# Edge loop of a graph attention layer: the running sum as a plain addition, its source slot read from a table

## What is computed

```python
def gnn(x, src, dst, edge_attr):             # x: normalised
    q, k, v = (x @ W + b for each)           # [N, 8, 32]
    e = edge_attr @ We                       # [E, 8, 32]
    alpha = sum(q[dst] * (k[src] + e)) / sqrt(32)
    ea = exp(alpha - segment_max(alpha, dst)[dst])
    denom = segment_sum(ea, dst)
    msg = (v[src] + e) * (ea / denom[dst])
    return segment_sum(msg, dst) + x @ Ws + bs
x = x + gnn(layernorm(x))
x = x + moe_top2_of_8(layernorm(x))          # router, two experts per node, relu, 256 -> 512 -> 256
```

## Time and profile before

| | us |
|---|---|
| median of three runs | 2544.61 |
| the profiled execution's own time | 2543.3 |
| its span, first to last instruction | 2541.5 |
| PE busy | 2375.7 (93%) |
| DVE busy | 2029.1 (80%) |
| POOL busy | 1809.0 (71%) |
| ACT busy | 1573.9 (62%) |
| edge loop, first L1050 to last | 227.4 to 1927.0 |
| mean granted TensorE clock | 0.966 of full speed |

### The profile page before, as it was taken

The page is one execution under the profiler, slowest core; times in us unless marked ns, Lnnn a source line. Parts: engine busy times, 40 slices in busy tenths (PEclk is TensorE's granted clock), DMA queues, the critical chain, the costliest instruction groups (busy, mean ns, idle before and its releaser), DMA issues. The chain is left out here.

```text
span 2541.5 us, 61885 instructions
## 1 busy us (share of the span) xinstructions
PE 2375.7 (93%) x13314; PEld 1998.8 (79%) x13315; DVE 2029.1 (80%) x5248; ACT 1573.9 (62%) x4349; POOL 1809.0 (71%) x2136
## 2 busy tenths in 40 slices
PE   6998999999999999999999999999996658999998
PEld 3445888888888888888888888888884647999998
DVE  6865999999999999999999999999997873222222
ACT  1223677776777677777777777776775115666665
POOL 4213788888888888888888888888886204666666
PEclk9999999999999999999999999999998558999999
DMA  7326777777777777777778777777772672433443
GB/s 233 129 106 197 234 229 224 228 228 224 223 228 228 219 229 228 223 228 226 228 226 230 228 223 228 226 228 215 230 225 82 203 215 57 71 63 64 69 67 54
DMA packets 337727, 476.35 MB, mean 187 GB/s; under 512 B 61382, under 2 KB 268556, under 8 KB 337116
## 3 DMA queue, kind: packets, MB, share of 16 engines
q0 software_dynamic: 92576, 259.72, 38.4%
q1 hardware_dynamic: 238556, 213.23, 27.7%
q10 hardware_dynamic: 6288, 0.05, 0.1%
HBM read 425.40 MB, written 50.57 MB: 187 GB/s over the span
## 5 line engine op out<-in xcount | busy, mean ns | idle before, releaser
L809 POOL DMA_INDIRECT kv_ring<-vk_table,tab_c x880 | 860.0, 977 | 274.9 <-issue 176.5
L967 PE MATMUL ps_e<-we_sb,aT 128*128 128x256 f32 x3520 | 917.8, 384 | 23.8 <-DVE ve_ke L1055 19.9
L967 PEld LDWEIGHTS ps_e<-we_sb,aT 128*128 128x128 f32 x3520 | 602.0, 191 | 95.6 <-issue 46.3
L1050 DVE TENSOR_TENSOR ve_ke<-kv_ring,ps_e 128x512 f32<-128x512 f32 x880 | 599.7, 681 | 34.1 <-PE ps_e L971 22.7
L819 POOL TENSOR_TENSOR ve_ke<-ve_ke 128x256 f32<-128x256 f32 x880 | 551.2, 630 | 16.5 <-ACT factor L936 3.0
L1020 PE MATMUL ps_u<-ve_ke,sel 128*128 128x264 f32 x1760 | 545.3, 392 | 17.0 <-POOL ve_ke L819 6.1
L971 PE MATMUL ps_e<-q_slots,selT 128*128 x1760 | 517.5, 375 | 0.0
L896 ACT COPY aT<-ps_t 128x256 f32<-128x256 f32 x880 | 325.4, 370 | 294.6 <-PE ps_t L951 255.3
L1126 DVE SCALAR_TENSOR_TENSOR node_slots<-node_slots,same_tile,ps_u 128x264 f32 x880 | 422.6, 480 | 25.5 <-PE ps_u L1020 21.4
L971 PEld LDWEIGHTS ps_e<-q_slots,selT 128*128 128x128 f32 x1760 | 335.3, 191 | 45.1
L1038 DVE TENSOR_REDUCE alpha<-ve_ke 128x8 f32<-128x256 f32 x880 | 362.4, 412 | 1.9
(11 more groups left out here) (251 smaller groups left out, 2630.3 us busy)
## 6 DMA issues: line engine op xcount, KB each, us to landing
a_ring<-in_edge_attr SPq DMA_DIRECT2D x880, 128.0 KB
loc_c<-loc_table SPq DMA_DIRECT2D x220, 128.0 KB, 4.4
kv_ring<-vk_table,tab_c POOLq DMA_INDIRECT x880
vk_table<-kv_out SPq DMA_DIRECT2D x49, 256.0 KB, 2.0
skip_table<-skip_out SPq DMA_DIRECT2D x49, 128.0 KB, 1.7
skip<-skip_table SPq DMA_DIRECT2D x7, 896.0 KB, 9.3
xn_table<-node_slots SPq DMA_DIRECT2D x7, 896.0 KB, 5.1
w_sb<-in_L_ffn_W SPq DMA_DIRECT2D x2, 2048.0 KB, 10.3
```

The lines of the kernel that those rows point to most:

```text
L809: g.indirect_dma_start(out=kv_ring[:, i % N_KV, :], out_offset=None, in_=vk_table, in_offset=bass.IndirectOffsetOnAxis(ap=tab_c[:, c % N_T ...
L967: t.matmul(ps_e[i % 2][:, 0:D], aT[i % 2][:, k * P:(k + 1) * P], we_sb[:, k, :], start=(k == 0), stop=(k == KD - 1))
L1050: v.tensor_tensor(ve_ke[:, to:ke + 1:ke - to, 0:D], kv.rearrange("p (t d) -> p t d", t=2), e[:, None, :].to_broadcast([P, 2, D]), ALU.add) ...
```

## The change

The 0/1 factor goes out of the addition. A table made in the first stage gives for each item the pair (tile, source): source is the tile itself if the item before had the same tile, else NT + 2, a new slot behind the others whose 264 columns are zero. The table stands in two halves at partitions 64 and 96 of `item_rows`. The addition is a tensor_tensor of the source slot and `ps_u`. The registers are loaded for two items at once, four values, in `score` behind the key/value addition (L1050) of each item whose addition has an even index, that is at the odd items. In the drain, where there are no scores, the load stands ahead of the addition. Three small tables of the router stage and the output buffers `y` of the expert stage become parts of other buffers.

```diff
+        item_slots = [item_rows[64 + 32 * h:65 + 32 * h, :].rearrange("p (i k) -> p i k", k=2) for h in range(2)]
-        node_slots = sb("node_slots", [P, NT + 2, SLOT])
+        sums_flat = sb("node_slots", [P, (NT + 2) * SLOT + UW])
+        node_slots = sums_flat[:, 0:(NT + 2) * SLOT].rearrange("p (j w) -> p j w", w=SLOT)
...
+            from_rep = t_rep
...
                 g.memset(node_slots[:, 0, 0:UW], 0.0).then_inc(first_cleared, 1)
+                g.memset(sums_flat[:, (NT + 2) * SLOT:(NT + 2) * SLOT + UW], 0.0).then_inc(first_cleared, 1)
...
                 then(v.tensor_tensor(same_tile[:, 1:IT], node_tile_rep[:, 1:IT], node_tile_rep[:, 0:IT - 1], ALU.is_equal))
+                then(v.scalar_tensor_tensor(out=from_rep[:, :], in0=node_tile_rep[:, :], scalar=float(NT + 2), in1=same_tile[:, :],
+                                            op0=ALU.subtract, op1=ALU.mult))
+                for h in range(2):
+                    row, some = slice(64 + 32 * h, 65 + 32 * h), slice(h * IT // 2, (h + 1) * IT // 2)
+                    v.tensor_copy(item_slots[h][:, :, 0], node_tile_rep[row, some])
+                    then(v.tensor_scalar(item_slots[h][:, :, 1], from_rep[row, some], float(NT + 2), None, ALU.add))
...
-                def score(c, par, i):
+                def score(c, par, i, meanwhile):
...
                     v.tensor_tensor(ve_ke[:, to:ke + 1:ke - to, 0:D], kv.rearrange("p (t d) -> p t d", t=2),
                                     e[:, None, :].to_broadcast([P, 2, D]), ALU.add).then_inc(s["ve_added"], 1)
+                    meanwhile()
                     if i:
                         reduce(c, par, i - 1)
...
-                    some = slice(c * CH + h * HALF, c * CH + (h + 1) * HALF)
-                    return nc.values_load_multi_w_load_instructions(
-                        item_node_tile[0:1, some], engines=[mybir.EngineType.DVE], min_val=0, max_val=NT,
+                def slots_of(c, i):
+                    h, m = divmod(c * CH + i, IT // 2)
+                    both = nc.values_load_multi_w_load_instructions(
+                        item_slots[h][:, m:m + AT_ONCE, :].rearrange("p i k -> p (i k)"), engines=[mybir.EngineType.DVE],
+                        min_val=0, max_val=NT + 2, ...)[1]
+                    return list(zip(both[0::2], both[1::2]))
...
-                def add(c, i, n, before):
+                def add(c, i, n, source):
                     m = c * CH + i
-                    to, sofar = [sums_flat[:, bass.ds(k * SLOT, UW)] for k in (n, before)]
+                    to, sofar = [sums_flat[:, bass.ds(k * SLOT, UW)] for k in (n, source)]
                     dve.wait_ge(s["summed"], at("summed", m))
                     dve.wait_ge(s["acc_added"], at("acc_added", m - 1))
-                    v.scalar_tensor_tensor(out=to, in0=sofar, scalar=same_tile[:, m:m + 1], in1=ps_u[i % 2][:, 0:UW], op0=ALU.mult, op1=ALU.add
-                                           ).then_inc(s["acc_added"], 1)
+                    v.tensor_tensor(to, sofar, ps_u[i % 2][:, 0:UW], ALU.add).then_inc(s["acc_added"], 1)
...
+                    def load_next(place):
+                        if adds and place + len(adds) >= places:
+                            cc, k = adds.pop(0)
+                            if k % AT_ONCE == 0:
+                                ahead[:] = slots_of(cc, k)
...
-                            score(c, par, i)
+                            score(c, par, i, lambda: load_next(i))
...
-                            if i % HALF == 0 and not ahead:
-                                ahead[:] = node_tiles_of(c - back, i // HALF)
-                            n = ahead.pop(0)
-                            before = last_tile[0] if last_tile else n
+                            if not places:
+                                load_next(CH)
+                            n, source = ahead.pop(0)
                             if i == 0:
-                                rescale(c - back, before)
-                            add(c - back, i, n, before)
+                                rescale(c - back, last_tile[0] if last_tile else n)
+                            add(c - back, i, n, source)
...
-            held, taker, unused, parts = [sb5(n, [P, NB]) for n in ("held", "taker", "unused", "parts")]
+            parts = sb5("parts", [P, NB])
+            held, taker, unused = [others[:, :, :].rearrange("p j e -> p (j e)")[:, i * NB:(i + 1) * NB] for i in range(3)]
...
-            y = [sb7(f"y{i}", [P, D]) for i in range(4)]
+            y = [values[:, i, :] for i in range(4)]
```

More of the change, by code:

```diff
@@ L368, in _ @@
                         resets()
-                pool.wait_ge(first_cleared, 1)
+                pool.wait_ge(first_cleared, 2)
             @block.scalar
@@ L1109, in _ @@
                 last_tile, ahead = [], []
[L1110 to L1115, removed]
-                    some = slice(c * CH + h * HALF, c * CH + (h + 1) * HALF)
-                    return nc.values_load_multi_w_load_instructions(
-                        item_node_tile[0:1, some], engines=[mybir.EngineType.DVE], min_val=0, max_val=NT,
-                        skip_runtime_bounds_check_because="a count of at most NT steps")[1]
@@ L1121, in add @@
-                def add(c, i, n, before):
+                AT_ONCE = 2
+                assert CH % AT_ONCE == 0 and IT // 2 % AT_ONCE == 0
+                def slots_of(c, i):
+                    h, m = divmod(c * CH + i, IT // 2)
+                    both = nc.values_load_multi_w_load_instructions(
+                        item_slots[h][:, m:m + AT_ONCE, :].rearrange("p i k -> p (i k)"), engines=[mybir.EngineType.DVE],
+                        min_val=0, max_val=NT + 2, skip_runtime_bounds_check_because="a count of at most NT steps, or NT + 2")[1]
+                    return list(zip(both[0::2], both[1::2]))
@@ L1129, in emit @@
                 def emit(c, par, steps):
+                    adds = [(c - b, k) for kind, k, b in steps if kind == "add"]
+                    places = len([1 for kind, k, b in steps if kind == "score"])
+                    def load_next(place):
[3 more added lines that the diff above has]
+                                ahead[:] = slots_of(cc, k)
                     for kind, i, back in steps:
@@ L1136, in emit @@
                         else:
-                            if i % HALF == 0 and not ahead:
-                                ahead[:] = node_tiles_of(c - back, i // HALF)
-                            n = ahead.pop(0)
-                            before = last_tile[0] if last_tile else n
+                            if not places:
+                                load_next(CH)
+                            n, source = ahead.pop(0)
                             if i == 0:
-                                rescale(c - back, before)
-                            add(c - back, i, n, before)
+                                rescale(c - back, last_tile[0] if last_tile else n)
+                            add(c - back, i, n, source)
                             last_tile[:] = [n]
-                            if i % HALF == HALF - 1 and m_of(c - back, i) + 1 < NCH * CH:
-                                ahead[:] = node_tiles_of((m_of(c - back, i) + 1) // CH, (i // HALF + 1) % 2)
                 over_chunks(dve, emit, what="add", parts={3: "scan", 4: "scan_back", 6: "own", 7: "least", 8: "shift"})
@@ L1416, in gnn_ffn @@
             block = c5.enter_context(nc.Block())
-            assert NT * NE <= 512 and NE == 8 and NT % NQ == 0 and 3 * NB <= 512 and TOP == 2 and NBK <= P
+            assert NT * NE <= 512 and NE == 8 and NT % NQ == 0 and 3 * NB <= 512 and TOP == 2 and NBK <= P and 3 * NB <= NT * NE
             NQS = TOP * NT // NQ
@@ L1555, in _ @@
                                             in1=parts.rearrange("p (k b) -> p k b", k=TOP), op0=ALU.mult, op1=ALU.add))
-                then(v.tensor_scalar(taker[:, :], held[:, :], 1.0, 0.0, ALU.subtract, ALU.max))
-                v.tensor_copy(take_i[:, :], taker[:, :])
-                then(v.tensor_scalar(unused[:, :], held[:, :], 0.0, float(PAD_DST), ALU.is_equal, ALU.mult))
-                v.tensor_tensor(put_i[:, :], taker[:, :], unused[:, :], ALU.add)
+                then(v.tensor_scalar(taker, held, 1.0, 0.0, ALU.subtract, ALU.max))
+                v.tensor_copy(take_i[:, :], taker)
+                then(v.tensor_scalar(unused, held, 0.0, float(PAD_DST), ALU.is_equal, ALU.mult))
+                v.tensor_tensor(put_i[:, :], taker, unused, ALU.add)
             @block.sync
```

5 lines of the change are left out of this document (2 added, 3 removed).

## The result

The changed kernel takes 2522.82 us (median of four runs, 2519.88 to 2526.86) against 2545.75 of the kernel before in the same job: ratio 0.9909, 95% interval 0.9890 to 0.9927. The profiled execution took 2519.88, its span is 2518.1; it was the fastest of the four. A second job of five runs gave 2526.65 and 0.9928 (0.9914 to 0.9942). The lines of the edge loop move by nine or ten: L1050 is now L1059, L1038 L1047, L1055 L1065, L1126 L1135, L1103 L1113, L967 L976, L1020 L1029 and L819 L828; L1104 is now L1114.

What follows compares the result with a forecast made beforehand. PE and DVE were taken to pace the edge loop in turn, PE standing still up to 1.3 us a chunk. 2543.3 - 24.9 (additions) + 3.5 (table) = 2521.9, with 1.3 for the median 2523 us; range 2506 to 2548.

Steps and rivals of the forecast that it cites:

- What bounds the loop: Edge loop: PE and DVE lead in turn; PE's own work 29.6 us of a 30.9 us chunk, idle up to 1.3.
- The addition: DVE's addition of 264 columns in the edge loop: the plain form takes 62 to 63 ns less than 480.
- The rival by which the plain addition is no faster: Addition in the edge loop: both forms cost the same, only the table is left, 2548 us; chance 0.07.
- Eight additions on the path, 0.47 a chunk: Additions at items 13, 14, 15, 0 and 4 to 7 count: 0.47 us a chunk, 53 chunks, 24.9 us less.
- The other eight stand beside PE's 1.77 and only make DVE wait sooner: A chunk's remaining eight additions run beside PE's 1.77 us per item and save no time.
- The loads: Four-value register loads behind L1050 of odd items: about 430 ns each, hidden under its 0.60 us, cost zero.
- were one register step before and are again: DVE's queue in the edge loop: an addition's two addresses still take one register step; no cost was counted.
- The table: First stage, DVE operations just before the first statistics: 3.5 us more, bounds 0 and 5.
- Disturbed chunks: Transfers in the edge loop: items coming sooner can turn near misses into waits, 0 to 6 us, taken as 0.
- The rivals of more and of less on the path: Edge loop: all 16 additions count, 53 us less, chance 0.08; or only four, 13 us less, chance 0.12.

Runs made afterwards that it cites:

- experiment 8: Changed kernel with product and reduction on half of each head's columns, leaving out half of each score: 2493.77 us, 0.9803 of the kernel before.
- experiment 2: Changed kernel with the addition as scalar_tensor_tensor, its factor 1.0 in the instruction instead of read from SBUF: 2528.11 us, 0.9921 of the kernel before.
- experiments 3 and 4: Changed kernel with only the path's eight additions plain (3: 2532.38 us, 0.9941), or only the other eight (4: 2546.37 us, 1.0001); the rest with the SBUF factor.
- experiment 1: Changed kernel with the old scalar_tensor_tensor addition back, table, pair loads and source slots kept: 2550.39 us, 1.0015 of the kernel before.
- experiments 5 and 7: Changed kernel with the pair load directly ahead of its addition (5: 2562.08 us, 1.0063), or sixteen values per load behind the key/value addition (7: 2580.78 us, 1.0139).
- experiment 6: Changed kernel with each pair load meant to issue twice; the second was left out of the program, so the changed kernel ran again: 2525.28 us, 0.9919.

## Why the prediction was right, and where it was off

The time, 2522.82 against 2523, is nearer than the terms deserve. One by one:

- *What bounds the loop.* Right. PE's floor of 29.6 a chunk was an estimate from two lengths and comes out at about 29.5 (experiment 8); DVE holds the path between items 13 and 1 and between 4 and 8, and the two waits of PE shrank and stayed. The additions on the path are those named, but each belongs to an item 29 places back, and not 13: item 0 of the chunk before is added at item 13. That changes nothing in the count of 53 chunks.
- *The addition.* 62 or 63 ns less was said, 60 less a mean and 0.06 to the next start were found. The reason was only half seen. The rows compared two forms, and I read the difference as that of the form; experiment 2 puts it on the factor read from SBUF. For this change it is the same, for another it is not. The rival by which the plain addition is no faster is refuted (482 to 420). Of the rule that the Trainium skill has in Vector Engine (DVE) Microarchitecture Reference, Measured stream behaviour on trn2, half holds here: the plain form and the one with a constant factor do cost the same (420 and 421), but the factor from SBUF has a price of its own, 61, which one fixed cost leaves out.
- *Eight additions on the path, 0.47 a chunk.* Eight were right, and they carry 0.45 (experiments 3 and 4). "The other eight stand beside PE's 1.77 and only make DVE wait sooner" failed in one place: in the old form they let the rescaling begin 0.05 us earlier against POOL's weighing, and that costs 0.06 a chunk. So the plain addition saves 0.52. The kernel's net 0.47 is that less 0.05 that the rest of the change costs in the loop (experiment 1), a term that the prediction set at zero. Two errors of 3 us cancelled, which is luck.
- *The loads.* 343 ns and not 430, since the cost isn't linear between one value (303) and eight (597). They cost nothing behind L1059, which experiments 5 and 7 show from both sides. The floor of about 600 ns that the Trainium skill (DMA: Bandwidth & Descriptors, Latency and other measured facts) puts under a load does not show here: 338 was the least and 343 the median. 0.05 a chunk is the bound for all that is new in the loop together, and nearly all of it is not the loads but the address step. It lies in item 13 (2.71 before, 2.76 in experiment 1). There the step on DVE's queue that works out the two addresses stands behind the wait for the rescaling, and from the end of the rescaling to the addition it now takes 0.357 instead of 0.315 (medians). That they "were one register step before and are again" is right as a count, but the step got longer (queue rows before and after):

```profile
L1126 DVEq FUSED_REGOPS  x879: 57/57/57, 279.8 to 1952.6; - x176
```

```profile
L1135 DVEq FUSED_REGOPS  x880: 57/93/110, 280.9 to 1931.0; - x176
```

- *The table.* 3.5 us was said, 2.6 measured. The mis-sized term is the casts and scalings of 440: I took L498's 0.62, which reads PSUM, and the new ones, which read SBUF, take 0.37 to 0.40. Nearer rows stood in the same stretch of the kernel before, 880 columns from SBUF in the time that L498 needs for 440 from PSUM. The number of partitions isn't it, since L503 works on 128:

```profile
18.61 0.61 DVE L500 CAST item_rows<-node_tile_rep 1x880 int32<-1x880 f32 x1
...
20.35 0.62 DVE L503 TENSOR_SCALAR t_rep<-t_rep 128x880 f32<-128x880 f32 x1
```

- *Disturbed chunks.* Not in the sum, and the largest uncertainty of a single execution. The mean of the chunks lies 0.36 to 0.54 over the 10th percentile in the changed kernel, its repeats and the kernels of experiments 2 and 3, 19 to 28 us over the 52 distances: 30.61 in the changed kernel's profile, 30.71 in its second one, with the same 30.25 under both. Items make up 5.8 of the 8.5 us by which the two profiled executions differ (2519.88 and 2528.43). So that the medians, 2522.8, 2526.7 and 2525.3 for the repeat of experiment 6, lie at the point forecast or within 4 us of it is partly luck.

The rivals of more and of less on the path fall by the same runs: all 16 additions together save 0.52 a chunk, not 1.0, and the eight of the path 0.45, not 0.25.

## What to carry to other kernels

Where two engines are both full, find the stretches in which each leads before pricing a faster instruction: of 52.7 us taken off DVE, 24 came off the time, and that share could be read from the order of time of one chunk. A factor of 0 or 1 that a running sum reads per partition can become an address, and register loads are free only where the instructions already handed to the engine last longer than the load: here behind the 0.60 us of L1059, and not where the queue has just waited. And look at an instruction of one shape whose time spreads (416 to 743 ns): here its cause was a neighbour on another engine, and a factor kept in PSUM took it away.

## What the runs showed of the hardware

- A per-partition factor from SBUF adds 60 ns to a scalar_tensor_tensor of 264 columns: 482 to 421 with the factor in the instruction, 420 for tensor_tensor.
- A register load on DVE's queue takes 303 ns for one value, 343 for four, 597 for eight and 1100 for sixteen: 13 ns a value up to four, 63 a value from there.
- A DVE tensor_tensor of 256 columns with two SBUF inputs takes 418 ns alone and about 600 to 656 where POOL's tensor_tensor on SBUF overlaps its start by 0.31 to 0.36 us: wherever the overlap is 0.11 us or more it ends 0.28 to 0.30 us behind POOL's instruction. With the second input in PSUM it takes 411 to 421 in all cases. POOL's weighing keeps its 0.62 us.
- The same operation on eight columns takes 154 ns when it starts 0.06 us into POOL's gather, and about 578, until the gather's end, when it starts 0.4 us or more into it (experiment 7).
